# Attention scores: from three bfloat16 parts over 96 rows to two float32r parts in either 64-row half of the array

## The reference, cut to what matters

```python
q = (x @ Wq.T).reshape(B, L, H, dh)      # H = 16 heads, dh = 16
k = (x @ Wk.T).reshape(B, L, H, dh)
v = (x @ Wv.T).reshape(B, L, H, dh)
attn = jnp.einsum('blhd,bmhd->bhlm', q, k) / scale
p = jax.nn.softmax(attn, axis=-1)
o = jnp.einsum('bhlm,bmhd->blhd', p, v).reshape(B, L, D)
return o @ Wo.T
```

## Time and profile before

| | |
|---|---|
| median of 3 runs | 638.35 us (637.68 to 640.59) |
| profiled execution: its time, which is its span | 639.8 us |
| PE busy | 603.8 us, 94% |
| DVE busy | 410.2 us, 64% |
| ACT busy | 385.0 us, 60% |
| POOL busy | 139.0 us, 22% |
| mean granted TensorE clock | 0.984 of full |

### The profile page before, as it was taken

The page is one execution under the profiler, slowest core; times in us unless marked ns, Lnnn a source line. Parts: engine busy times, 40 slices in busy tenths (PEclk is TensorE's granted clock), DMA queues, the critical chain, the costliest instruction groups (busy, mean ns, idle before and its releaser), DMA issues.

```text
span 639.8 us, 9019 instructions
## 1 busy us (share of the span) xinstructions
PE 603.8 (94%) x3442; PEld 307.8 (48%) x3442; DVE 410.2 (64%) x548; ACT 385.0 (60%) x748; POOL 139.0 (22%) x128
## 2 busy tenths in 40 slices
PE   5796687999999999999999999999999999999998
PEld 4685254222222323233433332333323988888887
DVE  6341597788888888898888988988711553121122
ACT  3666254777777777776767777776887443222221
POOL 2144154000000000011050511221322464333223
PEclk9999599999999999999999999999999999999999
DMA  6127458400701501400500710110120000001010
GB/s 189 34 99 128 94 131 179 64 1 4 100 1 23 80 1 35 68 2 21 81 1 3 100 34 3 34 35 2 34 68 2 0 2 12 23 0 34 1 34 33
DMA packets 24709, 28.64 MB, mean 45 GB/s; under 512 B 4335, under 2 KB 17975, under 8 KB 24667
## 3 DMA queue, kind: packets, MB, share of 16 engines
q1 hardware_dynamic: 20395, 23.35, 18.9%
q10 hardware_dynamic: 4272, 4.72, 2.2%
HBM read 19.40 MB, written 8.59 MB: 44 GB/s over the span
## 4 chain that ended last, share of the span: by engine, by line
PE 82%; DVE 7%; DMA 4%; POOL 2%; ACT 2%; issue 1%; SPq 1%; ACTq 0%; DVEq 0%
PE psum L1058 23%; PE psum L1140 19%; PE psum L1126 18%; PE psum L1090 16%; DVE nmax L892 4%; PE psum L1032 4%; PE psum L1172 2%; POOL qk_parts L526 2%; DMA scr_qk<-qk_parts 2%; DMA k_st<-scr_qk 1%; DMA w_raw<-in_L_cond_Wo 1%; ACT prob L719 1%; DVE nmax_parts L872 1%; DVE xs L857 0%; SPq L442 0%
## 5 line engine op out<-in xcount | busy, mean ns | idle before, releaser
L719 ACT ACTIVATE prob<-psum 128x512 f32<-128x512 f32 x512 | 277.4, 599 | 100.2 <-PE psum L1126 91.6
L892 DVE TENSOR_REDUCE nmax<-psum 128x1 f32<-128x1024 f32 x256 | 303.2, 1219 | 49.0 <-PE psum L1090 46.6
L1090 PE MATMUL psum<-k_st,q_st 96*128 96x512 bf16 x512 | 155.7, 388 | 12.4 <-DMA k_st<-scr_qk 7.9
L1126 PE MATMUL psum<-q_st,k_st 99*128 99x512 bf16 x512 | 154.4, 383 | 5.4 <-ACT prob L719 5.4
L1140 PE MATMUL psum<-prob,v_sb 128*17 128x512 f32 x1024 | 134.9, 599 | 0.9 <-ACT prob L719 0.7
L1126 PEld LDWEIGHTS psum<-q_st,k_st 99*128 99x128 bf16 x512 | 49.0, 97 | 174.4 <-ACT prob L719 139.9
L1016 DVE TENSOR_TENSOR h_f<-psum,silu_g 128x512 f32<-128x512 f32 x32 | 22.1, 692 | 94.3 <-PE psum L1058 87.8
L1090 PEld LDWEIGHTS psum<-k_st,q_st 96*128 96x128 bf16 x512 | 46.3, 99 | 53.9 <-DVE nmax L892 13.9
L769 ACT ACTIVATE silu_g<-psum 128x512 f32<-128x512 f32 x32 | 19.1, 597 | 78.6 <-PE psum L1058 78.6
L591 POOL TENSOR_TENSOR h_lo<-h_f,h_hi 128x512 fp32r<-128x512 f32 x32 | 41.6, 1301 | 79.1 <-ACT h_hi L748 79.1
L1058 PE MATMUL psum<-yn_hi,fw_lo 128*128 128x512 f32 x128 | 50.7, 396 | 0.0
(11 more groups left out here) (131 smaller groups left out, 620.4 us busy)
## 6 DMA issues: line engine op xcount, KB each, us to landing
scr_qk<-qk_parts SPq DMA_DIRECT2D x16, 384.0 KB, 2.8
q_st<-scr_qk SPq DMA_DIRECT2D x48, 128.0 KB, 4.5
k_st<-scr_qk SPq DMA_DIRECT2D x48, 128.0 KB, 7.0
x_in<-in_x SPq DMA_DIRECT2D x3, 512.0 KB, 4.0
out_x<-attn SPq DMA_DIRECT2D x3, 512.0 KB, 2.9
f_raw<-in_L_cond_gate_w ACTq DMA_DIRECT2D x2, 512.0 KB, 3.4
f_raw<-in_L_cond_hid_w ACTq DMA_DIRECT2D x2, 512.0 KB, 3.4
f_raw<-in_L_cond_out_w ACTq DMA_DIRECT2D x2, 512.0 KB, 3.8
```

What stands on the lines that cost most here:

```text
L719: nc.scalar.activation(prob[e % PR][:, :], e_bank(e), ACT.Exp).then_inc(exp_done, 1)
L892: nc.vector.tensor_reduce(out=nmax[:, b, h, t:t + 1], in_=slot, axis=AX.XY, op=ALU.max, negate=True).then_inc(max_used, 1)
L1090: last = nc.tensor.matmul(slot[:, half, :], q_st[g % SLOTS][0:PROD_ROWS, h, lt * P:(lt + 1) * P], k_st[g % SLOTS][0:PROD_ROWS, h, half * 5 ...
L1126: nc.tensor.matmul(e_bank(e), k_st[g % SLOTS][0:ALL_ROWS, h, kt * P:(kt + 1) * P], q_st[g % SLOTS][0:ALL_ROWS, h, half * HALF:(half + 1) * ...
```

## The change

Q and K are cut into two float32r parts instead of three bfloat16 ones. Three products of parts are kept, so a head's stack has 48 rows, and with two parts of the maxima 50. Heads are stored in `PAIRS = 2` pairs: one head of a pair (`e = 0`) lies at partitions 0 to 49, the other (`e = 1`) at 64 to 113. A score or maximum matmul so addresses only the 64-row half in which its head lies. The bytes of a stack and the number of its loads stay the same (12 transfers of 128 KB). `part2`, `third_part` and `split_maxima` are gone; the second part is written in one operation (DVE for chunks 0 and 1, POOL for 2 and 3), and the maxima are transposed first and cut by two DVE operations after that. Scores of a step are made in the order of `HEAD_ORDER`, and the third score of a step is placed between the two matmuls of the first maximum unit (`max_around`).

```diff
-Q_PARTS = ((0, 3), (1, 2), (2, 1))
-K_PARTS = (0, 1, 2, 0, 1, 0)
+Q_PARTS = (0, 0, 1)
+K_PARTS = (0, 1, 0)
 PROD_ROWS = DH * len(K_PARTS)
-ALL_ROWS = PROD_ROWS + 3
+ALL_ROWS = PROD_ROWS + 2
+ROWS = 64
+PAIRS = GH // 2
...
-        q_st = [sb(f"q_st{i}", [P, GH, SEQ], bf16, scope_b) for i in range(SLOTS)]
+        q_st = [sb(f"q_st{i}", [P, PAIRS, SEQ], f32r, scope_b) for i in range(SLOTS)]
...
-        qk_parts = [sb(f"qk_parts{i}", [P, 3, CW], bf16, scope_p) for i in range(4)]
+        qk_parts = [sb(f"qk_parts{i}", [P, 2, CW], f32r, scope_p) for i in range(4)]
...
         def unit(u):
-            half, h, t = u % GU // HU, u % HU // QT, u % QT
-            return u // GU, h, half * QT + t
+            half, pair, t, e = u % GU // HU, u % HU // (2 * QT), u % (2 * QT) // 2, u % 2
+            return u // GU, e, pair, half * QT + t
+
+        def head_rows(e, n):
+            return slice(ROWS * e, ROWS * e + n)
+
+        HEAD_ORDER = ((1, 0), (0, 0), (0, 1), (1, 1))
...
             for i in range(SLOTS):
-                sp.dma_start(k_st[i][PROD_ROWS:ALL_ROWS, :, :],
-                             ones_row[:, :].unsqueeze(1).to_broadcast([3, GH, SEQ])).then_inc(ones_loaded, 16)
+                for e in range(2):
+                    sp.dma_start(k_st[i][ROWS * e + PROD_ROWS:ROWS * e + ALL_ROWS, :, :].bitcast(f32),
+                                 ones_row[:, :].unsqueeze(1).to_broadcast([2, PAIRS, SEQ])).then_inc(ones_loaded, 16)
...
             def save_parts(c, tiles=range(4)):
                 for j in tiles:
-                    sp.wait_ge(parts_ready, 4 * c + j + 1)
+                    if c < DVE_PARTS:
+                        wait_evacuated(sp, "QK", c, j)
+                    else:
+                        sp.wait_ge(parts_ready, 4 * (c - DVE_PARTS) + j + 1)
...
+                for w, (stack, parts) in enumerate(((q_st, Q_PARTS), (k_st, K_PARTS))):
+                    for i, part in enumerate(parts):
+                        src = scr_qk[w, part, ch, tok].rearrange("(p e d) t -> e d p t", e=2, d=DH)
+                        for e in range(2):
+                            row = ROWS * e + DH * i
+                            sp.dma_start(stack[g % SLOTS][row:row + DH, :, :].bitcast(f32), src[e]
+                                         ).then_inc(stack_loaded[g % SLOTS], 16)
...
-                sp.dma_start(q_st[slot][PROD_ROWS:ALL_ROWS, :, half * HALF:(half + 1) * HALF],
...
+                for e in range(2):
+                    sp.dma_start(q_st[slot][ROWS * e + PROD_ROWS:ROWS * e + ALL_ROWS, :, half * HALF:(half + 1) * HALF
+                                            ].bitcast(f32), src[e]
+                                 ).then_inc(max_loaded[NHALF * slot + half], 16)
...
-            def third_part(c, j):
-                n = 4 * c + j
-                pool.wait_ge(part2_ready, n + 1)
-                nc.gpsimd.tensor_tensor(qk_parts[j][:, 2, :], qk_rest[n % 3][:, :], qk_parts[j][:, 1, :],
-                                        ALU.subtract).then_inc(parts_ready, 1)
...
-            def part2(n):
-                c, j = n // 4, n % 4
...
-            def split_maxima(n, step):
...
                 elif what == "T":
                     if n:
                         dve.wait_ge(nmax_saved, 16 * n)
-                    nc.vector.tensor_copy(nmax_t[:, :], slot[0:3 * HU, 0, 0:P // 2].bitcast(bf16)).then_inc(max_used, 1)
+                    link(nc.vector.tensor_copy(nmax_t[:, 0, :], slot[0:HU, 0, 0:P]))
+                    nc.vector.tensor_tensor(nmax_t[:, 1, :], slot[0:HU, 0, 0:P], nmax_t[:, 0, :].bitcast(f32),
+                                            ALU.subtract).then_inc(max_used, 1)
...
+            def scores_to_max(item, half):
+                g, e, pair, lt = unit(item[1])
+                rows = head_rows(e, PROD_ROWS)
+                return nc.tensor.matmul(max_slot(item)[:, half, :], q_st[g % SLOTS][rows, pair, lt * P:(lt + 1) * P],
+                                        k_st[g % SLOTS][rows, pair, half * 512:(half + 1) * 512],
+                                        start=True, stop=True)
+
+            def max_around(item, step, i):
+
+                pe.wait_ge(max_used, max_no[item] - 1)
+                if item[1] % GU == 0:
+                    operands_loaded(item[1] // GU)
+                scores_to_max(item, 0)
+                scores(step, i)
+                scores_to_max(item, 1).then_inc(max_filled, 1)
...
                 elif what == "T":
-                    pe.wait_ge(nmax_split, n + 1)
-                    last = nc.tensor.transpose(slot[0:3 * HU, 0, 0:P // 2].bitcast(bf16),
-                                               nmax_parts[:, :, :].rearrange("p a q -> p (a q)"), ident_bf[:, :])
+                    wait_item(pe, "max", HU * n + HU - 1)
+                    last = nc.tensor.transpose(slot[0:HU, 0, 0:P],
+                                               nmax[:, n % 2, :, :, :].rearrange("p e a t -> p (e a t)"), ident[:, :])
...
-            def scores(s, h):
+            def scores(s, i):
                 g, half, kt = s // (NHALF * LT), s // LT % NHALF, s % LT
-                e = GH * s + h
-                if e >= EB:
-                    pe.wait_ge(exp_done, e - EB + 1)
...
+                n = GH * s + i
+                e, pair = HEAD_ORDER[i]
+                rows = head_rows(e, ALL_ROWS)
+                if n >= EB:
+                    pe.wait_ge(exp_done, n - EB + 1)
...
             for s in range(NSTEP + 1):
-                if s < NSTEP:
-                    for h in range(GH - 1):
-                        scores(s, h)
                 items = max_items(s) if s < NSTEP else []
                 early = 1 if items and items[0][0] == "max" else 0
-                for item in items[:early]:
-                    do_item(item)
+                if s < NSTEP:
+                    scores(s, 0)
+                    scores(s, 1)
+                    if early:
+                        max_around(items[0], s, 2)
+                    else:
+                        scores(s, 2)
                 if 1 <= s <= NSTEP:
                     values(s - 1)
```

More of the change, by code:

```diff
@@ L542, in _ @@
                     low_part(step[1])
-                elif step[0] == "QK" and step[1] < DVE_PARTS:
-                    third_part(step[1], step[2])
-                elif step[0] == "QK":
+                elif step[0] == "QK" and step[1] >= DVE_PARTS:
                     c, j = step[1:]
@@ L881, in item_of_max_slot @@
                 slot = max_slot(item)
-                if what == "max" and n >= HU:
-                    for step in {0: (0,), 1: (1,), 2: (2, 3)}.get(n % HU, ()):
-                        split_maxima(n // HU - 1, step)
-                elif what == "T" and n == NG * NHALF - 1:
-                    for step in range(4):
-                        split_maxima(n, step)
                 dve.wait_ge(max_filled, max_no[item] + 1)
                 if what == "max":
-                    b, h, t = n // HU % 2, n % HU // QT, n % QT
-                    nc.vector.tensor_reduce(out=nmax[:, b, h, t:t + 1], in_=slot, axis=AX.XY, op=ALU.max,
+                    b, (_, e, pair, t) = n // HU % 2, unit(n)
+                    t %= QT
+                    nc.vector.tensor_reduce(out=nmax[:, b, e, pair, t:t + 1], in_=slot, axis=AX.XY, op=ALU.max,
                                             negate=True).then_inc(max_used, 1)
@@ L1083, in do_item @@
                         pe.wait_ge(evacuated[i], before_items[i])
[L1084 removed]
                 if what == "max":
[L1086 removed]
                     if n % GU == 0:
[L1088 to L1092 removed]
+                        operands_loaded(n // GU)
+                    scores_to_max(item, 0)
+                    last = scores_to_max(item, 1)
                 elif what == "T":
[L1094 to L1096 removed]
+                    wait_item(pe, "max", HU * n + HU - 1)
+                    last = nc.tensor.transpose(slot[0:HU, 0, 0:P],
+                                               nmax[:, n % 2, :, :, :].rearrange("p e a t -> p (e a t)"), ident[:, :])
                 elif what == "O":
@@ L1138, in values @@
                         pe.wait_ge(o_cleared, 1)
-                for h in range(GH):
+                for i, (e, pair) in enumerate(HEAD_ORDER):
+                    h = 2 * pair + e
                     last = nc.tensor.matmul(O_BANK[32 * h:32 * h + VW, :], v_sb[:, b * LT + kt, hg * GH + h, :],
-                                            prob[(GH * s + h) % PR][:, :], start=kt == 0, stop=kt == LT - 1)
+                                            prob[(GH * s + i) % PR][:, :], start=kt == 0, stop=kt == LT - 1)
                 last.then_inc(pv_done, 1)
```

107 lines of the change are left out of this document (26 added, 81 removed).

## The result

The changed kernel took 662.73 us in the median of four executions (three of 660.12 to 663.76 us and one of 703.12) against 638.82 us before (637.68 to 640.59, four executions) on the same chip: a ratio of 1.0367, 95% interval 1.0316 to 1.0417. Forecast were 623.0 us, range 612 to 650. The three that are compared have their median at 661.69 us, so the kernel is slower by 23 us, and the forecast had the wrong sign.

A forecast was written before the change was run, and what follows sets the result against it. PE was taken to bound the loop (busy 94%), with DVE next at 2.52 us of a 2.82 us step. Loop -8.2 and preparation -7.5 took 639.8 to 624.1 us; the median, 1.4 lower, gave 623, range 612 to 650.

The forecast's parts named there:

- The plain step: Loop step with maxima and no item: 2.82 to 2.69 us, a gain of 0.13 in each of 81 steps.
- What is late next: Loop, score 2's wait for score 3's exponential: stays hidden with score 2 at about 1.15 us, binding only 0.08 us sooner.
- the term of 0.02 for close loads: Plain loop step, after score 1: two loads into the same half follow closely, adding 0.02 us.
- Items of full shape: Loop steps with full-height items: two shape changes at 0.10 us each; 33 steps lose 2.3 us in all.
- The last steps: Last 14 loop steps: the wait for the exponential, then values, sets the step, so a faster score 1 gives 0.
- Preparation: Stage before the loop: less POOL, ACT and DVE work moves the loop's start from 110.3 to about 103.5; -7.5 us taken.
- the last save: End of preparation: its 5.22 us shrink to about 3, landing near 103 us.
- a granted clock that falls in the loop: Sign of being wrong, in the loop: the granted clock falls because PE has become idle; no size given.
- no overlap: Rival, loop: score 1 starts a full gap after score 0, a step is 2.91 us, 648 us in all; chance 0.20.
- Preparation gives little: Rival, preparation: slower saves or loads, or maxima alone setting its end, give 2.9 us or less; 628 to 631 us; chance 0.13.
- Free shape changes: Rival, loop items: changes between 64 and 128 rows cost nothing, all else as forecast; 616 us; chance 0.12.
- Loads that wait for a computing half: Rival, loop: six gaps within a half expose 188 ns loads, a step 1.13 us longer, about 750 us; chance 0.05.

The follow-up runs named there:

- experiment 4: Changed kernel with score and maximum matmuls reading the upper two bytes of each element as bf16, same halves and order: 634.44 us, ratio 0.9926 to the kernel before.
- experiment 1: Changed kernel with both matmuls of the first maximum unit placed before score 2: 648.15 us, ratio 1.0135 to the kernel before.
- experiment 10: Changed kernel with the exponential over 384 of 512 columns, the remaining probabilities left at one: 656.05 us, ratio 1.0267 to the kernel before.
- experiment 3: Changed kernel with score and maximum matmuls over all rows instead of halves, summing two heads, stacks cleared first: 665.03 us, ratio 1.0364 to the kernel before.
- experiment 6: Kernel before (three bf16 parts, full height) with only the new order, score 2 between the first unit's matmuls: 641.97 us, ratio 1.0023 to the kernel before.
- experiment 2: Changed kernel with the heads' halves swapped, scores 0 to 3 in halves 0, 1, 1, 0: 636.75 us, ratio 0.9967 to the kernel before.
- experiment 5: experiment 2 with the 28 maximum units of preparation at full height, summing two heads: 627.01 us, ratio 0.9795 to the kernel before.
- experiment 8: experiment 2 with preparation's 28 maximum units at full height through zero-padded stationary copies, computing everything: 629.89 us, ratio 0.9851 to the kernel before.
- experiment 9: Changed kernel, order and halves kept, with preparation's 28 maximum units at full height, summing two heads: 654.87 us, ratio 1.0268 to the kernel before.

## Why the prediction was wrong

**The plain step: forecast 2.69, measured 2.83.** The step that failed is "What is late next": "In the new order score 2 comes at about 1.15 us, so this wait stays hidden", together with the term of 0.02 for close loads. I had priced float32r where loads are hidden, 0.23 us from one matmul to the next, and that holds. Where nothing hides the load, after values and after every wait, a float32r matmul is 0.50 us long and the next follows 0.34 later, 0.11 more than between hidden loads; in bf16 it is 0.40 and 0.24 (experiment 4). The exponential therefore starts 0.54 instead of 0.42 us after score 3, and frees the bank at 1.19 instead of 1.07. I had put score 2 at 1.15, 0.08 us from the point at which the wait binds, and it bound. Behind it follow a second bare load, 0.34 us to the unit matmul that the change puts there, and 0.32 to values. The terms against my 2.69: +0.04 for score 2's start and +0.11 for its load, which is the 0.14 to within 0.01. (The float32r term of the sum was rounded down besides: seven times 0.23 - 0.216 is 0.10, not 0.07; it did not matter, since the wait set the step.) Experiments 1, 4 and 10 each take away one link of this chain and give 0.17, 0.20 and 0.11 us a step; experiment 3 shows that the halves are not to blame, experiment 6 that the order alone isn't.

The price could have been read in the trace of before, where the feed-forward layer begins behind values, PE:

```profile
492.32 0.50 PE L1058 MATMUL psum<-yn_hi,fw_lo 128*128 128x512 f32 x1
492.66 0.39 PE L1058 MATMUL psum<-yn_lo,fw_hi 128*128 128x512 f32 x1
```

**Items of full shape: forecast +0.07 each, measured +0.5** (`O` 3.26 to 3.77, forecast 3.33). This was the largest error of the loop, +15.5 us where I had +2.3. (There are 32 such steps with maxima, 14 with `O` and 18 placed by hand; I had counted 19 of the latter.) The term priced PE's time for the item and two changes of shape. The step hangs on a handshake instead: score 3, `O` on PE, DVE frees the slot, the next unit, score 2, unit, values. Three prices lie on it, and the runs take them apart:

- The order alone, in experiment 6: 3.26 to 3.38, +0.12. Score 2 now stands behind DVE's release instead of ahead of it: from the unit to values 0.23 us more, up to the release 0.11 less.
- float32r at full height and in the new order, in experiment 3: 3.38 to 3.63, +0.25. Score 3 to `O` goes from 0.23 to 0.34 us, and from the unit that waited for DVE to values it is 0.90 instead of 0.76: two loads that nothing hides.
- Half height, from experiment 3 to the changed kernel: 3.63 to 3.77, +0.14. Score 3 to `O` goes from 0.34 to 0.42, and the second of the four transposes follows the first after 0.16 instead of 0.11. With bf16 halves (experiment 4) score 3 to `O` is 0.33, where bf16 at full height has 0.23.

So a change between 64 and 128 rows costs PE about 0.1 us, as I had taken it, but only the one ahead of the item lies on the chain; the other two prices I had not seen. A bare load costs the same 0.11 here as in the plain step.

**The last steps: forecast 0, measured +0.2 each** (2.39 to 2.59), two bare loads on the chain score 3, exponential, score 2, values; in bf16 they are back at 2.40.

**Preparation: forecast -7.5, measured -0.9.** The work that I removed did go: in the five kernels with the changed preparation as it stands (the changed kernel, experiments 1, 2, 4 and 10) the first maximum is reduced at 63.7 to 65.6 us, in the two with the preparation of before at 66.14 and 69.32. Two steps failed. One is the silent assumption that PE stays out of the way in the row of maxima. With half-height units the clock was at 1.2 GHz for 20 to 27 us of it (in experiments 1 and 2 with a break of 3 to 7 us), and the row took 44.1 to 46.3 us; with full-height units at 7 to 10 us of low clock it took 36.9 to 37.7 (experiments 3, 5, 8 and 9), before 38.0. The other is the last save: I had it shrink from 5.22 us to about 3, and it took 4.9 after and 5.2 in experiment 5. The first exponential starts 0.2 us after it has landed in each of these traces, and its tiles are made by PE between the units, so a long row puts it off. ACT after, to lay beside the earlier trace rows:

```profile
109.38 2.08 ACT L699 ACTIVATE prob<-psum 128x512 f32<-128x512 f32 x4 [1.51 <-DMA scr_qk<-qk_parts]
```

With full-height units the same preparation ends at 100.98 and 101.67 us (experiments 5 and 9), against 107.66 to 109.92 in the five kernels with half-height ones and 106.46 and 110.32 with the preparation of before. So 5 to 9 us could be had, and the clock took them back; that my -7.5 lies between is in part luck, since 2 us of it were the save that did not shrink. The same happens at the loop's beginning, where the clock is low until 116.8 us (before, until 114.7): +1.3 us in the first step. In the loop after that the clock is full, so that my sign "a granted clock that falls in the loop" was wrong about the place.

**Sum:** +1.3 - 0.9 + 1.7 + 6.8 + 8.7 + 2.0 in the loop, -0.9 before it, -0.2 behind it: +18.5 us, the difference of the spans. The medians of the executions compared differ by 22.9 us. An execution's time is 1.8 us more than its span (660.12 and 658.3 us), so the median spans are near 659.9 us after and 637.0 before: the profile after lies 1.6 us under its median and that of before 2.8 over.

**Right were** the overlap of the halves, the 0.23 us of float32r in a stream, POOL freed of L526, and the feed-forward stage at its length. Of the rivals, *no overlap* had the right sign by a mechanism that did not occur. *Preparation gives little* came true: it had named the maxima as what might set the end, but not the clock that lengthens their row. *Free shape changes* did not come true (0.1 us, above). *Loads that wait for a computing half* did not either: units of the same half follow one another by 0.23 us. Of the signs of being wrong, two showed: plain steps over 2.82 us, and score 2 waiting for ACT.

## What to carry to other kernels

A matmul has two prices, in a stream and behind a wait: before a type with slower loads goes into a loop, count the waits on the chain of its step, give each the higher price, and distrust a next wait that is nearer to binding than one load. Price an item in a ring of two slots by its handshake (writer, reader, next writer, and what is queued behind that), not by its time on PE. Where row halves are used, put neighbours into different halves (a ratio to the kernel before of 0.9967 instead of 1.0367 by one line here), and look at the granted clock wherever half-height matmuls run, even where full-height ones stand between them.

## What the runs showed of the hardware

**Row halves run at the same time without slowing each other**, and a matmul starts ahead of others that stand before it in the program when its half is free: score 1 started 0.04 us after score 3, while a unit matmul (0.35) and score 0 (0.81) that precede it came later. It did not pass one that waited for another engine: in experiment 2 a unit matmul with a free half started only with score 2 ahead of it, 0.6 us after the pair before. The Trainium skill ("TensorE: Matmul & The Clock Gate", Part 3) says that matmuls start and end strictly in program order. For the starts this trace does not agree; the exponentials still came in the order of the scores, so the completion counts may well have been in order.

**The height of matmuls bears on the clock**: in the same place of the same program the granted clock stood at 0.50 with units of 48 rows (17 to 27 us in six kernels) and rose to 1.00 within 7 us with units of 112 rows (three kernels; 10 us in experiment 3). What in the array makes it so is not known from these runs.

**A float32r load of 50 x 128 that nothing hides costs 0.11 us** more than a hidden one; a bf16 one 0.01 to 0.02.

**A change between 64 and 128 rows costs about 0.1 us**: from a score to the transposes behind it PE took 0.23 us in bf16 at full height, 0.33 in bf16 halves, 0.34 in float32r at full height and 0.42 in float32r halves.
